# A 54-score search without its shift, and small scales given to GpSimd, in a four-block decoder on one core

## The reference, cut to what matters

```python
# second mixer (per head h): gates of a recurrence, decayed scores
log_f = log_sigmoid(fg); F = cumsum(log_f)
D = exp(F_s - F_t + ig_t - max); C = (q @ k.T) / 4 * D
h = C / max(|C.sum|, exp(-max)) @ v; layernorm per head
# third feed-forward: quantised tokens and hidden values, ternary weights
xq = round(x / s), s = max|x| / 127 + 1e-5
y = (xq @ wq) * s * ws
out = qlinear(silu(qlinear(x, w_gate)) * qlinear(x, w_up), w_down)
# fourth mixer: only the 54 largest scores of a row count
scores = coef * Q @ K_mem.T                       # 256 tokens x 256 keys
scores = scores - max(scores)
thr = top_k(scores, 54)[..., -1:]
att = softmax(where(scores < thr, -inf, scores)); out = att @ V_mem @ W_o.T
# fourth feed-forward: as the third, with square(relu(h)) between two products
out = bitlinear(square(relu(bitlinear(x, w1))), w2)
```

## Time and profile before

| what | us |
|---|---|
| runs shown | 565.84, 568.44, 562.04 (median 565.84) |
| profiled execution, its time | 569.39 |
| its span, first to last instruction | 567.7 |
| TensorE busy | 461.2 (81%) |
| VectorE busy | 355.7 (63%) |
| ScalarE busy | 234.0 (41%) |
| GpSimd busy | 145.7 (26%) |
| mean granted TensorE clock | 0.901 |

### The profile page before, as it was taken

One profiled execution on the slowest core, in us unless ns is written; L12 is line 12 of the kernel. 1 busy time (PEld: TensorE's weight loads), 2 busy tenths in 40 slices (PEclk: granted clock), 3 DMA queues, 4 the chain that ended last, 5 costly groups with the idle time before them and its releaser, 6 DMA issues.

```text
span 567.7 us, 7522 instructions
## 1 busy us (share of the span) xinstructions
PE 461.2 (81%) x2709; PEld 339.5 (60%) x2718; DVE 355.7 (63%) x987; ACT 234.0 (41%) x422; POOL 145.7 (26%) x139
## 2 busy tenths in 40 slices
PE   1899989999999837779889689999887754766775
PEld 0688875557787625445556457788664533654544
DVE  6473456639314546695656668246478899799753
ACT  1200013532242715354543212423888643225896
POOL 4000010064854675433064555001000000010000
PEclk9999987999899968777798689999999996897978
DMA  8840260025894410001000200000000000000001
GB/s 269 273 186 1 72 224 1 1 68 193 307 286 133 145 53 17 7 5 38 0 1 2 76 1 1 1 0 1 0 2 0 1 1 0 2 1 0 10 29 38
DMA packets 21078, 34.70 MB, mean 61 GB/s; under 512 B 4935, under 2 KB 16074, under 8 KB 21040
## 3 DMA queue, kind: packets, MB, share of 16 engines
q1 hardware_dynamic: 18736, 30.23, 15.8%
q0 software_dynamic: 2304, 3.97, 2.5%
HBM read 32.32 MB, written 4.19 MB: 64 GB/s over the span
## 4 chain that ended last, share of the span: by engine, by line
PE 46%; DVE 30%; ACT 11%; POOL 6%; issue 5%; DMA 1%; DVEq 0%; POOLq 0%; ACTq 0%
PE bank L1516 5%; PE bank L1475 5%; PE bank L1485 5%; PE bank L1592 4%; PE bank L1847 3%; PE bank L1861 2%; DVE bnst L613 2%; DVE HN L623 2%; PE bank L1614 2%; DVE top L1137 2%; POOL ar L568 2%; DVE big L1134 2%; PE bank L1668 2%; DVE am L1019 2%; DVE X L824 1%
## 5 line engine op out<-in xcount | busy, mean ns | idle before, releaser
L471 POOL TENSOR_TENSOR rstd<-ve,neghalf 128x2 f32<-128x2 f32 x32 | 23.3, 729 | 270.0 <-DVE ve L618 269.9
L954 DVE TENSOR_TENSOR SH<-bank,HM 128x512 f32<-128x512 f32 x32 | 21.8, 688 | 23.2 <-ACT HM L1315 10.6
L1315 ACT ACTIVATE HM<-bank 128x512 f32<-128x512 f32 x32 | 19.1, 597 | 36.5 <-PE bank L1701 29.3
L623 DVE TENSOR_SCALAR HN<-X,mv,rstd 128x256 f32<-128x256 f32 x64 | 28.6, 488 | 7.8 <-POOL rstd L471 7.6
L1592 PEld LDWEIGHTS bank<-ph,big 128*128 128x128 f32 x256 | 31.9, 196 | 1.3 <-issue 0.4
L1475 PE MATMUL bank<-HM,CT 128*128 128x256 f32 x128 | 30.7, 403 | 1.2 <-DVE HM L647 1.2
L568 POOL TENSOR_TENSOR ar<-ar,neghalf 128x32 f32<-128x32 f32 x4 | 21.7, 5432 | 38.7 <-DVE ar L918 38.7
L1516 PE MATMUL bank<-HT,SH 128*128 128x512 f32 x64 | 31.6, 645 | 0.0
L1592 PE MATMUL bank<-ph,big 128*128 128x64 f32 x256 | 31.2, 276 | 0.0
L1475 PEld LDWEIGHTS bank<-HM,CT 128*128 128x128 f32 x128 | 26.0, 204 | 5.6 <-issue 1.5
L613 DVE BATCH_NORM_STATS2 bnst<-X 128x6 f32<-128x256 f32 x64 | 24.0, 418 | 7.6 <-POOL X L580 6.8
(11 more groups left out here) (364 smaller groups left out, 1160.7 us busy)
## 6 DMA issues: line engine op xcount, KB each, us to landing
big<-in_ew SPq DMA_DIRECT2D x16, 768.0 KB, 6.5
y_rows<-ph SPq DMA_DIRECT2D x16, 128.0 KB, 3.2
X<-in_x SPq DMA_DIRECT2D x4, 256.0 KB, 6.7
CT<-in_ctxT SPq DMA_DIRECT2D x1, 1024.0 KB, 7.7
CN<-in_ctx SPq DMA_DIRECT2D x1, 1024.0 KB, 11.4
ar<-in_q2g SPq DMA_DIRECT2D x1, 1024.0 KB, 4.9
ar<-in_q2u SPq DMA_DIRECT2D x1, 1024.0 KB, 7.1
big<-in_q2d SPq DMA_DIRECT2D x1, 1024.0 KB, 10.1
```

Source lines behind the costliest of these rows:

```text
L471: pool.tensor_tensor(rstd[:, b, :], ve[:, b, :], neghalf[:, 0:TB], ALU.pow)\
L623: last = dve.tensor_scalar(HN[:, TB * b + j, :], X[:, TB * b + j, :], mv[:, b, j, 0:1], rstd[:, b, j:j + 1], ALU.subtract, ALU.mult)
L954: dve.tensor_tensor(cs[:, g, :], bank[i % 3][:], dcs[:, i % 2, :], ALU.mult).then_inc(s["s_cs"], 1)
L1315: act.activation(dcs[:, i % 2, :], bank[4 + i % 2][:], ACT.Exp).then_inc(s["s_dexp"], 1)
```

## The change

It has five parts and a new order.

- **Opening of the head loop.** TensorE's and ScalarE's four `VC` folds go ahead of the first token turn; `rows_turn(0)`, `spread_rows(0)` and `turned_rows(0)` go into the first round, behind its scores. VectorE takes `token_norm(0)` and `gathered(2)` ahead of the weight scales, and `gathered(3)` behind the row chain. `compose_rows` waits for each of the three parts by itself.
- **Search without the shift.** VectorE searches in the raw scores. ScalarE makes the exponentials with the negative maximum as bias, half by half, and then shifts the scores itself; VectorE shifts the 54th score by one small sum and masks as before.
- **Rectification halved.** In `in3` ScalarE rectifies the first 512 columns, VectorE the other 512. A new step `max3` holds the hidden maximum (VectorE), the square (ScalarE) and the output scale (GpSimd).
- **Token scales on GpSimd.** `fg` is made on GpSimd; both users wait for it.
- **Output scales on GpSimd.** `fy1` is made on GpSimd; the last addition waits for it.
- **New order.** All four strings of `TURNS_OF` are new; GpSimd's list grows from 22 to 46 steps, VectorE's from 92 to 100, ScalarE's from 126 to 134.

```diff
...
-        (("in2a", "TVS"), ("in2b", "TVS"), ("round2", "S"), ("turn2", "TS"), ("out2", "TV" if j < TB - 1 else "TVG"))]
+        (("in2a", "TVS"), ("in2b", "TVSG"), ("round2", "S"), ("turn2", "TS"), ("out2", "TV" if j < TB - 1 else "TVG"))]
...
-        (("in3", "TVS"), ("round3", "S"), ("turn3", "TS"), ("out3", "TV"))]
+        (("in3", "TVS"), ("max3", "VSG"), ("round3", "S"), ("turn3", "TS"), ("out3", "TV"))]
...
-          ("norm4", "TVS"), ("keys2", "TS"), ("values2", "TS"), ("scores2", "TVS"), ("probs2", "TS"), ("mix2", "TVG"), ("norm5", "VS"), ("turn5", "TS")] + FFN2 +
+          ("norm4", "TVS"), ("keys2", "TS"), ("values2", "TS"), ("scores2", "TVS"), ("probs2", "TS"), ("mix2", "TVG"), ("norm5", "VSG"), ("turn5", "TS")] + FFN2 +
...
-          ("project3", "TVG"), ("norm7", "VS"), ("turn7", "TS")] + FFN3)
+          ("project3", "TVG"), ("norm7", "VSG"), ("turn7", "TS")] + FFN3)
...
-    "T": ("00101021210200213031132031230122313020310232130130120120132310320212010203311321232323201013"
-          "30312201120333021201032321233031022313"),
-    "V": ("00121200213123033221303011200321213030120123102032112030321231323203101320213302013213203123"),
-    "S": ("00121200031231013021102320102331020313102112032013203120213102302030123211323213210102333201"
-          "0213031302120123230230313120232313"),
-    "G": ("2223031323012301230123"),
+    "T": ("00101021210201023110130210231023203123013321020130212102313021021323020301212331030322021131"
+          "33313122021013313202033202323131023023"),
+    "V": ("00121200211233013220031133020112023102102133020231213003213213020131321313210201332123030202"
+          "32331203"),
+    "S": ("01021200130121010120303201213023102130112202310231021021332302032013123010323021213131233011"
+          "322111030330201210232312332300322013323023"),
+    "G": ("2223031320101310221203301232031031123203120323"),
...
-        FULL = [("in2b", j) for j in range(TB)] + IN3
+        CUTS = ["scores3", "clip3"]
+        MAX3 = [("max3", j) for j in range(TB)]
+        FULL = [("in2b", j) for j in range(TB)] + MAX3
...
+                if step in QUANTS:
...
+                    f = QUANTS.index(step)
+                    pool.wait_ge(s["s_qs"], nth("V", QUANTS, step, b))
+                    for w in range(2 - f):
+                        last = pool.tensor_scalar(fg[:, TB * b:TB * (b + 1), w], sx[:, TB * b:TB * (b + 1)],
+                                                  wsc[:, 3 * f + w:3 * f + w + 1], None, ALU.mult)
+                    last.then_inc(s["s_fg"], 1)
+                if step in FULL:
...
+                    f = 0 if step[0] == "in2b" else 1
+                    pool.wait_ge(s["s_rh"], nth("V", FULL, step, b))
+                    pool.tensor_scalar(fy1[:, b:b + 1], sh1[:, b:b + 1], wsc[:, 2 + 2 * f:3 + 2 * f], tg[:, 6 + f:7 + f],
+                                       ALU.mult, ALU.mult).then_inc(s["s_fy"], 1)
...
-                link(dve.tensor_copy(part[p0:p1, 0, :], CG[p0:p1]))
+                dve.tensor_copy(part[p0:p1, 0, :], CG[p0:p1]).then_inc(s["s_part"], 1)
+                dve.wait_ge(s["s_part"], 3 * r + 1)
...
-                link(dve.tensor_copy(part[p0:p1, 1, :], rest[p0:p1]))
+                dve.tensor_copy(part[p0:p1, 1, :], rest[p0:p1]).then_inc(s["s_part"], 1)
+                dve.wait_ge(s["s_part"], 3 * r + 2)
...
+            token_norm(0)
+            gathered(2)
...
-            token_norm(0)
-            gathered(2)
...
-            gathered(3)
...
+            gathered(3)
...
-                if i in (0, 9, 18, 23):
-                    weighted_values((0, 9, 18, 23).index(i))
+                if i in (1, 9, 18, 23):
+                    weighted_values((1, 9, 18, 23).index(i))
...
-                for w in range(2 - f):
-                    dve.tensor_scalar(fg[:, t0:t1, w], sx[:, t0:t1], wsc[:, 3 * f + w:3 * f + w + 1], None, ALU.mult)
...
-                link(dve.tensor_scalar(fy1[:, w], sh1[:, w], wsc[:, 2 + 2 * f:3 + 2 * f], tg[:, 6 + f:7 + f],
-                                       ALU.mult, ALU.mult))
...
+                    dve.wait_ge(s["s_fg"], nth("G", QUANTS, "norm5", b))
...
-                    dve.wait_ge(s["s_gs"], nth("S", INS, step, b))
...
+                    dve.wait_ge(s["s_gu"], nth("T", INS, step, b))
+                    dve.wait_ge(s["s_fg"], nth("G", QUANTS, "norm7", b))
+                    dve.tensor_scalar(GS[b][:, 512:1024], bank_b(b)[:], fg[:, TB * b + step[1], 0:1], 0.0, ALU.mult,
+                                      ALU.max).then_inc(s["s_gv"], 1)
+                if step[0] == "max3":
+                    dve.wait_ge(s["s_gv"], nth("V", IN3, ("in3", step[1]), b))
+                    dve.wait_ge(s["s_gs"], nth("S", INS, ("in3", step[1]), b))
...
+                    dve.wait_ge(s["s_fy"], nth("G", FULL, ("in2b" if step[0] == "out2" else "max3", step[1]), b))
...
-                    link(dve.tensor_scalar(nmax2[:, b], top3[:, b, :, 0], -1.0, None, ALU.mult))
-                    for j in range(TB):
-                        dve.tensor_scalar(top3[:, b, j, :], top3[:, b, j, :], nmax2[:, b, j:j + 1], None, ALU.add)
-                    for j in range(TB):
-                        last = dve.tensor_scalar(SC[b][:, j, :], SC[b][:, j, :], nmax2[:, b, j:j + 1], None, ALU.add)
-                    last.then_inc(s["s_m3"], 1)
+                    dve.tensor_scalar(nmax2[:, b], top3[:, b, :, 0], -1.0, None, ALU.mult).then_inc(s["s_m3"], 1)
...
-                    dve.wait_ge(s["s_m3"], nth("V", ["scores3"], "scores3", b))
+                    dve.wait_ge(s["s_m3"], nth("V", CUTS, "scores3", b))
...
-                            done[j] = mark(dve.match_replace(WR[b][:, j, :], top3[:, b, j, :], src[:, j, :], LOWEST))
+                            last = dve.match_replace(WR[b][:, j, :], top3[:, b, j, :], src[:, j, :], LOWEST)
+                            if r >= 1:
+                                done[j] = mark(last)
+                        if r == 0:
+                            last.then_inc(s["s_m3"], 1)
+                            dve.wait_ge(s["s_m3"], nth("V", CUTS, "clip3", b))
...
-                            dve.wait_ge(s["s_vec"], done[j])
+                            if r >= 1:
+                                dve.wait_ge(s["s_vec"], done[j])
...
+                    at = (CLIP - 1) % 8
+                    for j in range(TB):
+                        dve.wait_ge(s["s_vec"], done[j])
+                    link(dve.tensor_tensor(top3[:, b, :, 0], top3[:, b, :, at], nmax2[:, b], ALU.add))
...
-                    at = (CLIP - 1) % 8
-                    for j in range(TB):
-                        dve.wait_ge(s["s_vec"], done[j])
+                    for j in range(TB):
...
-                                                        scalar=top3[:, b, j, at:at + 1], in1=EX3[b][:, j, :],
+                                                        scalar=top3[:, b, j, 0:1], in1=EX3[b][:, j, :],
...
+            for b in range(B):
+                folded(2 + B + b, VC[b])
...
-                act.wait_ge(s["s_part"], min(b, 2) + 1)
...
+                    act.wait_ge(s["s_part"], 3 * min(b, 2) + p + 1)
...
-            for b in range(B):
-                folded(2 + B + b, VC[b])
...
-            spread_rows(0)
-            turned_rows(0)
...
+                if i == 0:
+                    spread_rows(0)
+                    turned_rows(0)
...
+                    act.wait_ge(s["s_fg"], nth("G", QUANTS, "norm5", b))
...
-                    for n in range(2):
-                        last = act.activation(GS[b][:, 512 * n:512 * (n + 1)], bank[2 * b + n][:], ACT.Relu,
-                                              scale=fg[:, TB * b + step[1], 0:1])
-                    last.then_inc(s["s_gs"], 1)
-                    act.wait_ge(s["s_gs"], nth("S", INS, step, b))
+                    act.wait_ge(s["s_fg"], nth("G", QUANTS, "norm7", b))
+                    act.activation(GS[b][:, 0:512], bank_a(b)[:], ACT.Relu, scale=fg[:, TB * b + step[1], 0:1])\
+                        .then_inc(s["s_gs"], 1)
+                if step[0] == "max3":
+                    act.wait_ge(s["s_gs"], nth("S", INS, ("in3", step[1]), b))
+                    act.wait_ge(s["s_gv"], nth("V", IN3, ("in3", step[1]), b))
...
-                        act.wait_ge(s["s_sq"], nth("S", IN3, ("in3", step[1]), b))
-                    act.wait_ge(s["s_rh"], nth("V", FULL, ("in2b" if step[0] == "round2" else "in3", step[1]), b))
+                        act.wait_ge(s["s_sq"], nth("S", MAX3, ("max3", step[1]), b))
+                    act.wait_ge(s["s_rh"], nth("V", FULL, ("in2b" if step[0] == "round2" else "max3", step[1]), b))
...
-                    act.wait_ge(s["s_m3"], nth("V", ["scores3"], "scores3", b))
-                    act.activation(EX3[b], SC[b], ACT.Exp).then_inc(s["s_ex3"], 1)
+                    act.wait_ge(s["s_m3"], nth("V", CUTS, "clip3", b))
+                    for j in range(TB):
```

(13 more changed lines are left out.)

4 lines of the change are left out of this document (2 added, 2 removed).

## The result

| | kernel before | changed kernel |
|---|---|---|
| median, us | 563.98 (4 runs, 562.04 to 568.44) | 550.34 (547.26 to 560.30) |
| ratio, 95% interval | | 0.9716 (0.9648 to 0.9784) |
| profiled execution: time, span | 569.39, 567.7 | 549.89, 548.1 |
| mean granted clock | 0.901 | 0.922 |

The forecast was 554, range 547 to 565.

The account below looks back on a forecast made before the run. No engine alone sets the pace: VectorE bounds the search, ScalarE mostly the tail, written order between. Terms 2.8 + 5.0 + 4.6 = 12.4 us; 565.84 - 12.4 + 0.6 for small waits = 554, range 547 to 565.

Parts of the forecast that it names:

- Opening, 2.8: Opening of the head loop: second token turn at 224.4 instead of 227.1, taken as 2.8 us gained, bounds 0 to 4.4.
- The rival "clock": Opening: folds just ahead keep the gates at the upper clock, 1.6 us better, 552; chance counted within the forecast's 0.56.
- the folds fill the hole before 207 ... so they cost nothing: Opening: TensorE has nothing from 200 on, so the moved value folds, ending at 203.7, cost nothing.
- the 0.7 for the gathered rows: Opening: moving gathered rows 3 behind VectorE's row chain gains 0.7 us.
- VectorE up to the last mask, 5.0: VectorE until batch 3's mask: net 3.5 us less work plus 1.5 of idle time, 5.0 us gained, bounds -3 to 13.
- I take 1.5 of it: VectorE's idle time before the last mask: the new order saves 1.5 us of it, within 0 to 10.
- Drain, 4.6: From the last mask to the end: rectification halved and new orders, 4.6 us gained, bounds 0 to 10.
- The 42.4: Drain: going through three written orders step by step, the end comes 42.4 us behind the mask instead of 47.0.
- Scales on GpSimd, nothing on the path: Token and output scales moved to GpSimd: covers of about 3.3 and 4 us hide them, so no cost on the path.
- ScalarE's four pieces: Search: ScalarE's exponentials per half and score shifts, at most 0.55 us each, cost nothing, up to 1.5 per batch if late.
- The orders give nothing: Rival 1: waits in the new order eat the moved work; 2 to 6 us gained, 560 to 564; chance 0.26.
- Slower: Rival 3: the GpSimd round trip lands on the path, 24 scales at 0.83 cost 20 us, 574; chance 0.08.

Follow-up runs that it names:

- idle matmuls: Changed kernel plus 8 idle matmuls ahead of the first token turn and 28 between first gates and first exponents; ratio 0.9733 to the kernel before.
- the run with the folds back: Changed kernel with the four value folds behind the first gates again and their copies behind the first logarithm; ratio 0.9839 to the kernel before.
- the opening alone: Kernel before with only the new opening of the head loop; ratio 0.9891 to the kernel before.
- The order alone: Changed kernel with its orders and opening, but score shift, both rectified halves and scales made as before; ratio 0.9897 to the kernel before.
- late scales: Changed kernel with a spare 128x8 power ahead of each of GpSimd's 24 scales, 1.65 us late; ratio 0.9935 to the kernel before.

## Why the prediction was right, point by point

The time was right. Of its three terms the opening was too small, the stretch to the last mask too large, and the drain right for a reason that was only partly so. That 12.4 comes so near the 11.9 counted above is in part luck: the opening gave 1.9 more than its term, the drain 0.7 more, the stretch 3.1 less.

**Opening, 2.8.** Right in mechanism; 3.4 with the gates at the low clock, 4.7 with them at the high one. The rival "clock" (1.6 better) is 1.4 in the gates, and comes in some executions. In all eleven profiles with the folds just ahead and no idle matmuls the turn less the gates is 14.2 to 14.4 us, before 17.6, so the gates' clock is all that differs there. It goes with the hole ahead of the turn, for which the prediction took 3.4 us and the low level. In five profiles the hole was 2.24 to 2.52 us and the first gate ran at the upper level (all eight took 1.91 us three times, 2.74 and 3.02 where the clock fell while they ran); in six it was 3.62 to 4.30 us and the first gates ran at the lower level (3.25 to 3.58). The step that was off is "the folds fill the hole before 207 ... so they cost nothing": right for TensorE, but on ScalarE their copies had stood just ahead of the parts' copies (the last from 219.31 for 0.60 us, the parts' from 220.10). By the run with the folds back, less the 0.35 us of its slower gates, their new place is 1.4 to 2.2 us of the gain; the 0.7 for the gathered rows could not have come without it. On the clock the Trainium skill (TensorE: Matmul & The Clock Gate, What's actually happening) would have activity just ahead hold the upper level. The runs show both: 1.91 us behind 2.24 us without a matmul, and 3.62 behind 2.15 in the run with idle matmuls, each with TensorE busy right ahead.

**VectorE up to the last mask, 5.0.** This is the term that was mis-sized: 1.9 to 2.1 against the kernel before, 0.9 to 1.2 against the opening alone. Where it went can be read from the waits of VectorE in that stretch. Before (columns: total, times, longest):

```profile
DVE big L1092 <- ACT big L1408: 9.0, 4, 5.6
DVE nmax L1076 <- PE bank L1883: 7.9, 3, 5.7
DVE WK L1066 <- PE bank L1847: 7.9, 3, 4.4
DVE X L1071 <- PE bank L1861: 5.9, 3, 2.4
DVE HN L623 <- POOL rstd L471: 4.5, 7, 0.8
DVE top L1118 <- ACT big L1437: 2.4, 1, 2.4
```

and after:

```profile
DVE big L1107 <- ACT big L1436: 10.5, 6, 4.0
DVE nmax L1090 <- PE bank L1915: 9.8, 3, 7.7
DVE HN L640 <- POOL rstd L474: 7.5, 10, 0.8
DVE X L1085 <- PE bank L1893: 6.6, 3, 2.6
DVE WK L1080 <- PE bank L1879: 6.2, 2, 4.5
```

With the smaller rows the sums are 44.0 and 45.2 us. VectorE's work fell by 193.0 - 44.0 - (191.2 - 45.2) = 3.0 (its busy time alone by 3.6, 143.7 to 140.1), near the 3.5 that were predicted net. But "I take 1.5 of it" for its idle time was wrong by sign: the wait for scores (L1118 before) is gone as foreseen, while those for the gate, for the second attention's scores and for the deviation grew, and idle time rose by 1.2. So the three operations are worth a third to half of their durations here (shift 0.8 to 1.2 for 2.4, scales 1.3 to 1.7 for 3.7). The group put ahead of the mask was priced at 2.6 and costs 3.5.

**Drain, 4.6.** 5.3 to 5.5, but "ScalarE behind the last mask: rectification is halved" was the lesser half of the reason. The order alone gives 4.0 to 4.8 (47.0 or 47.8 to 43.0), the halving on top of it 1.6, and the new operations without the new order lose 2.0 to 2.8. The 42.4 was right because it came from going through the written orders, and not from ScalarE's 10 us.

**Scales on GpSimd, nothing on the path.** Right. The new rows (columns: line, engine, operation, tiles x count, busy, mean ns, idle time before):

```profile
L602 POOL TENSOR_SCALAR fy<-sh,wsc,tg 128x1 f32<-128x1 f32 x16 | 5.8, 366 | 66.9 <-DVE rh L1042 66.9
...
L1436 ACT ACT_TABLE_LOAD x4 | 5.1, 1283 | 0.7 <-POOL fg L595 0.6
...
L1118 DVE TENSOR_SCALAR big<-bank,fg 128x512 f32<-128x512 f32 x6 | 4.5, 749 | 1.6 <-PE bank L1956 1.3 <-issue 0.3
...
L1441 ACT ACTIVATE big<-bank,fg 128x512 f32<-128x512 f32 x6 | 4.1, 683 | 1.4 <-PE bank L1956 1.4
...
L595 POOL TENSOR_SCALAR fg<-sx,wsc 128x2 f32<-128x2 f32 x12 | 3.5, 297 | 7.6 <-DVE rq L1029 7.6
...
L1470 ACT ACTIVATE big<-big,nmax 128x256 f32<-128x256 f32 x6 | 2.7, 500 | 0.4 <-DVE big L1152 0.3
```

One product takes 0.30 to 0.37 us, not the 0.73 taken; one ScalarE wait of 0.6 is put to `fg`, and none of VectorE's. VectorE's took 0.23 and 0.26, so GpSimd is 1.3 to 1.4 times slower at one or two elements a lane; the 2.6 of the Trainium skill (GPSIMD Engine Reference, Elementwise - side-by-side cycle accounting), a figure per element that it gives for `tensor_tensor`, isn't seen in these `tensor_scalar`s of one or two elements. What the text gave as the price if the cover is gone, 0.83 for each user, left a victim out: with late scales the longest wait was that for a deviation behind them in GpSimd's queue.

**ScalarE's four pieces.** Nothing, as predicted: 0.5 us each, and the mask doesn't wait for them.

**Rivals.** "The orders give nothing" is out for the drain and holds for the stretch. "Slower" needed scales that their users wait for; one is, for the 0.6 us above.

## What to carry to other kernels

Work taken off a busy engine between two waits on others came through at a third to half of its duration here; look in the waits for what is late next before counting it in full. Splitting a step between two engines pays only if the in-order queue of the second reaches its half in time: the new operations gave 1.5 us of the drain in one order and cost 2.0 to 2.8 in another. When a small operation moves to another engine, ask who stands behind it in that engine's queue, besides who uses its result.

## What the runs showed of the hardware that I had not expected

In 9 of 14 profiles TensorE's clock had a mean of 0.77 between 79 and 101.5 us. In the kernel before (columns as in the windows above):

```profile
78.00:82.00 4.00, 2.06 (x17) 1.82 (x18) 2.21 (x9) 1.60 (x3) 0.79 (x1) 1.00 0.48 163
82.00:92.20 10.20, 10.20 (x31) 7.14 (x31) 5.94 (x23) 0.00 (x0) 0.00 (x0) 0.50 0.02 8
```

It stood at the lower level for some 10 us in which TensorE had no break, right behind 4 us in which TensorE was busy 2.1. In the profile of the changed kernel TensorE was busy 1.8 of the same 4 us, and the clock stayed at 1.00; what decides between the two, no run here shows. The fall is worth some 5 us, and 2 more behind it, half of what the change gave. And a clock that had just been high outlasted a hole of 2.2 to 2.5 us and the gates behind it in three executions, fell during the gates in two, and had fallen before them in the run with idle matmuls.
